# A hybrid block on one core: statistics by halves, W1 staged in W2's memory, weight peaks one per step, splits behind the tangents, and the first half's routing ahead of the last groups' additions

## The reference, cut to what matters

```
x = x + angles(layernorm(x))      # layer norm, l2 norm; s = clip(Q K^T) with 512 keys,
                                  # B = (1 - arccos(s)/pi)^9; l2norm(B @ q_weight) + bias
x = x + moe(layernorm(x))         # 8 experts of 128-512-128, top 2 of 8, plus a shared one, exact gelu
x = x + linear_attention(layernorm(x))   # 16 heads of 8, elu + 1
x = x + moe(layernorm(x))         # the same weights again
```

## Time and profile before

| what | us |
| --- | --- |
| median of 3 runs (lowest to highest) | 670.29 (667.02 to 672.75) |
| profiled execution: its time | 669.43 |
| its span, first to last instruction | 667.7 |
| busy in the span: PE / DVE / ACT / POOL | 489.1 / 515.2 / 450.7 / 366.1 |
| mean granted TensorE clock, as a share of full speed | 0.921 |

### The profile page before, as it was taken

The page is one execution under the profiler, slowest core; times in us unless marked ns, Lnnn a source line. Parts: engine busy times, 40 slices in busy tenths (PEclk is TensorE's granted clock), DMA queues, the critical chain, the costliest instruction groups (busy, mean ns, idle before and its releaser), DMA issues.

```text
span 667.7 us, 13526 instructions
## 1 busy us (share of the span) xinstructions
PE 489.1 (73%) x3817; PEld 354.5 (53%) x3817; DVE 515.2 (77%) x1200; ACT 450.7 (67%) x841; POOL 366.1 (55%) x382
## 2 busy tenths in 40 slices
PE   1276822874786987899957787866767999999770
PEld 1132302874332457788846566644332479999560
DVE  3988671588789547899889598776786769999992
ACT  1269999796562556899948578855642579999660
POOL 6023100333577777777747522237778737777673
PEclk9999975998698999899979999979896999999896
DMA  8800000004023453455581114102235324446943
GB/s 274 231 15 0 1 0 0 1 1 127 25 77 107 115 129 74 110 100 106 121 164 49 65 64 127 31 14 76 77 105 122 85 63 100 101 100 139 216 129 135
DMA packets 111961, 59.68 MB, mean 89 GB/s; under 512 B 76538, under 2 KB 101076, under 8 KB 111892
## 3 DMA queue, kind: packets, MB, share of 16 engines
q1 hardware_dynamic: 102804, 40.07, 25.2%
q0 software_dynamic: 9088, 18.76, 9.7%
HBM read 16.27 MB, written 23.90 MB: 60 GB/s over the span
## 4 chain that ended last, share of the span: by engine, by line
POOL 22%; issue 21%; DVE 16%; PE 16%; ACT 12%; SPq 9%; DMA 3%; POOLq 0%; DVEq 0%; ACTq 0%
POOL routed_rows L775 11%; POOL expert_results L821 6%; SPq L607 5%; SPq L616 2%; DMA side<-expert_results 2%; PE PA L1194 2%; DVE big L2084 2%; ACT SC L877 2%; DVE BN L1427 2%; DVE side L2098 2%; PE PA L1157 1%; DVE X L1645 1%; DVE peaks L1531 1%; SPq L605 1%; POOL RS L721 1%
## 5 line engine op out<-in xcount | busy, mean ns | idle before, releaser
L821 POOL DMA_INDIRECT expert_results<-side,DG x156 | 162.9, 1044 | 66.8 <-issue 47.0
L775 POOL DMA_INDIRECT routed_rows<-big,SLQ x128 | 143.1, 1118 | 57.2 <-issue 44.6
L1407 PE MATMUL PC<-W,big 128*128 x624 | 118.9, 277 | 27.5 <-DVE side L2098 27.1
L1097 ACT ACTIVATE SC<-PA,B1T,scl 128x256 f32<-128x256 f32 x208 | 100.8, 576 | 20.5 <-PE PA L1391 15.1
L2087 DVE SCALAR_TENSOR_TENSOR big<-SC,scl,big 128x1024 f16<-128x1024 f32 x78 | 100.2, 1284 | 2.8
L1409 PE MATMUL PC<-W,big 128*128 x468 | 87.6, 222 | 0.0
L1407 PEld LDWEIGHTS PC<-W,big 128*128 128x128 f16 x624 | 58.6, 99 | 38.7 <-issue 32.6
L2084 DVE TENSOR_SCALAR big<-SC,scl 128x1024 f16<-128x1024 f32 x78 | 67.4, 864 | 5.8 <-ACT SC L1097 5.8
L1107 ACT ACTIVATE big<-PC,DG 128x128 f32<-128x128 f32 x156 | 50.4, 390 | 19.3 <-PE PC L1407 10.4
L721 POOL TENSOR_TENSOR RS<-VA,halfneg 128x4 f32<-128x4 f32 x24 | 27.0, 1127 | 66.0 <-DVE VA L1679 65.9
L1097 ACT ACTIVATE SC<-PB,B1T,scl 128x256 f32<-128x256 f32 x104 | 50.7, 583 | 10.7 <-DVE big L2087 7.5
(11 more groups left out here) (288 smaller groups left out, 1188.7 us busy)
## 6 DMA issues: line engine op xcount, KB each, us to landing
big<-PB SPq DMA_DIRECT2D x32, 256.0 KB, 3.0
side<-expert_results SPq DMA_DIRECT2D x16, 512.0 KB, 4.1
routed_rows<-pad_zeros SPq DMA_DIRECT2D x23, 128.0 KB
expert_results<-side,DG POOLq DMA_INDIRECT x156
X<-n_L_attn_a_hidden_states SPq DMA_DIRECT2D x2, 1024.0 KB, 7.0
big<-in_L_ffn_w SPq DMA_DIRECT2D x1, 2048.0 KB, 8.4
routed_rows<-big,SLQ POOLq DMA_INDIRECT x128, 2.8
out_x<-X SPq DMA_DIRECT2D x8, 256.0 KB, 2.3
```

The costliest lines, as they stand in the source:

```text
L775: pool.indirect_dma_start(routed, bass.IndirectOffsetOnAxis(ap=SLQ[:, slot, t, c:c + 1], axis=0), XHL[:, slot, t, c, :].bitcast(I32), None ...
L821: pool.indirect_dma_start(results, bass.IndirectOffsetOnAxis(ap=DG[:, k, r, 0:1], axis=0), YT[:, k, r, :], None).then_inc(result_stored[k] ...
L1097: ins = act.activation(HF[:, k % 3, b * RU:(b + 1) * RU], up_out(k, b), ACT.Gelu, scale=INV1, bias=B1T[:, bass.ds(b1_at + b, 1)])
L1407: last = pe.matmul(both, hh, W2[:, :, at], start=(b == 0), stop=(b == HB - 1))
```

## The change

Nothing of what is computed changes. In the setup:

- K's weights are loaded ahead of X's second half, and POOL takes the inverse norms of K ahead of its last twelve constants. ACT loads its root table first of all.
- The first block's statistics are done by halves of 16 tiles: variances, first and second roots and the first two normalisations of half 0 come ahead of the statistics of X's second half; half 1's steps are spread over steps 1 to 4 of the score loop.
- The transposed K, attention weights and b1 are copied by ACT, out of other banks. W1 is staged in the memory where W2's parts will lie.

In the score loop the weight peaks come one per step (16 steps from step 3), and W1's splits leave it. Behind the last tangent DVE does the small peaks, the scales, W1's split and W2's split. POOL's reduction over partitions, and with it its bias additions, comes behind the peaks.

At the end of the value phase DVE does `choose(0)`, `place(0)` and `rows(0)` ahead of `first_add` of groups 6 and 7, and POOL puts single tiles of group 0's scatter between the roots and scalings of these groups. PE's and ACT's lists follow.

```
-        w1_stage = big[:, 0:WE]
+        w1_stage = W2[:].rearrange("p a n -> p (a n)").bitcast(F32)
...
                 sp.dma_start(grouped[:, mine, :, :], x_view[:, mine, :, :]).then_inc(s[name], 16)
-            sp.dma_start(KW[:], k_w.rearrange("(b p) d -> p b d", p=P)).then_inc(s["kw_loaded"], 16)
+                if not half:
+                    sp.dma_start(KW[:], k_w.rearrange("(b p) d -> p b d", p=P)).then_inc(s["kw_loaded"], 16)
...
-                    for g in range(NG - 1):
+                    for g in range(NG - 2):
                         x_scale(g)
                         group_root(g, 1)
+                    x_scale(NG - 2)
+                    scatter(0, 0, 0, (0,))
+                    group_root(NG - 2, 1)
+                    scatter(0, 0, 0, (1,))
                     x_scale(NG - 1)
-                    scatter(0, 0, 0, (0,))
+                    scatter(0, 0, 0, (2,))
                     group_root(NG - 1, 1)
-                    scatter(0, 0, 0, (1, 2, 3))
+                    scatter(0, 0, 0, (3,))
                     scatter(1, 0, 1)
...
+            act.preload_act_table(ACT.Abs_reciprocal_sqrt)
...
+            root(1)
+            act.wait_ge(s["setup_t"], 1)
+            act.activation(KT[:], PBk[0][:], ACT.Copy).then_inc(b_read[0], 1)
+            root(2)
             act.wait_ge(s["consts_made"], CONSTS)
-            root(1)
-            root(2)
+            act.wait_ge(s["setup_t"], 2)
+            act.activation(WOT[:], PA[1][:, 3 * P:4 * P], ACT.Copy).then_inc(s["wot_copied"], 1)
+            act.activation(WQKVT[:], PA[1][:, 0:3 * P], ACT.Copy).then_inc(a_read[1], 1)
+            act.wait_ge(s["setup_t"], 3)
+            act.activation(B1T[:], PA[0][:, 0:(E + 1) * HB], ACT.Copy).then_inc(a_read[0], 1)
...
             for n in range(NA + 3):
                 g = n // 2
-                if n == HI_AT:
-                    act.wait_ge(s["scales_made"], SCALE_STEPS)
-                if 0 <= n - HI_AT < CHUNKS // 2:
-                    weight_hi(n - HI_AT)
...
+                if n == 2:
+                    root(3)
                 score_angles(n - 3)
+                if n == 3:
+                    root(4)
...
                     act.preload_act_table(ACT.Gelu)
+                    gap(0)
                     gate_normalise(NG - 3)
                     gate_hi(NG - 3)
                     value_squares(NG - 1)
-                    gap(0)
+                    early_gelu(0)
+                    gate_turn(NG - 3)
                     gate_normalise(NG - 2)
                     gate_hi(NG - 2)
-                    gate_turn(NG - 3)
-                    early_gelu(0)
                     early_gelu(1)
...
                     route(0)
+                    early_up(0)
                     gate_rows_turn(NG - 3)
                     gate_logits(NG - 4)
-                    early_up(0)
                     early_up(1)
...
             for g in range(NG // 2):
                 bn(0, g)
+            variances(0)
             dve.wait_ge(s["kw_loaded"], 16)
             dve.wait_ge(s["k_rs"], 1)
...
+            first_roots(0)
+            second_roots(0)
...
+            for g in range(2):
+                normalise_a(g, 0, g)
+            dve.wait_ge(s["x_second"], 16)
+            for g in range(NG // 2, NG):
+                bn(0, g)
+            PEAKS_AT = 3
             for n in range(NA + 4):
                 g = n // 2
+                if n == 1:
+                    variances(1)
                 if n >= 4:
                     tangent(n - 4, (n - 4) // 4, (n - 4) % 4)
                 if n % 2 == 0 and 0 < g <= NG:
                     query(g - 1, (g - 1) // 2, (g - 1) % 2)
+                if n == 2:
+                    first_roots(1)
+                if n == 4:
+                    second_roots(1)
+                if n % 2 == 0 and 0 < g < NG - 1:
+                    normalise_a(g + 1, (g + 1) // 2, (g + 1) % 2)
+                if 0 <= n - PEAKS_AT < 2 * NG:
+                    largest_weight(n - PEAKS_AT)
+            small_peaks()
+            dve.wait_ge(s["peak_made"], 2 * NG)
+            dve.tensor_reduce(amax[:, 0:2], peaks[:], AX.X, ALU.max).then_inc(s["amax_made"], 1)
+            scales()
+            split_weights(W1H, W1L, w1_stage, S1, 0)
+            dve.wait_ge(s["w_split"], CHUNKS // 2)
+            split_weights(W2H, W2L, w2_stage, S2, CHUNKS // 2)
...
+                    gate_logits(NG - 5)
+                    choose(0)
                     sum_squares(NG - 2)
                     first_shift(NG - 3)
-                    gate_logits(NG - 5)
+                    place(0)
+                    rows(0)
                     first_add(NG - 2)
-                    choose(0)
+                    gate_lo(NG - 3)
                     sum_squares(NG - 1)
-                    gate_lo(NG - 3)
                     first_shift(NG - 2)
-                    place(0)
                     first_add(NG - 1)
-                    rows(0)
                     gate_logits(NG - 4)
```

More of the change, by code:

```diff
@@ L379, in build @@
         per = NG // 2
-        USES = [("setup", (0, 0), (1, 1), (1, 0)),
+        USES = [("setup", (1, 1), (1, 0), (0, 0)),
                 ("query", (0, 0), (per, per), (per, per)),
@@ L486, in build @@
         CONSTS, SCALE_STEPS, TABLE_STEPS, SMALL = 39, 10, 10, 10
-        def roots(norm):
-            return norm + 2
         xt_turned = [s[f"xt_turned{i}"] for i in range(RING)]
@@ L840, in _ @@
         def _(act):
+            act.preload_act_table(ACT.Abs_reciprocal_sqrt)
             def root(n):
+                tiles = slice((n - 1) // 2 * HT, ((n - 1) // 2 + 1) * HT)
                 act.wait_ge(s["var_ready"], n)
-                act.activation(EST[:], VA[:], ACT.Abs_reciprocal_sqrt).then_inc(s["root_ready"], 1)
+                act.activation(EST[:, tiles], VA[:, tiles], ACT.Abs_reciprocal_sqrt).then_inc(s["root_ready"], 1)
             act.wait_ge(s["kw_loaded"], 16)
@@ new lines, in step, with first_tiles, variances @@
+            def step(ins):
+                stat_steps[0] += 1
+                ins.then_inc(s["stat_step"], 1)
+                dve.wait_ge(s["stat_step"], stat_steps[0])
+            def first_tiles(half):
+                return slice(half * HT, (half + 1) * HT)
+            def variances(half):
+                h = first_tiles(half)
+                dve.wait_ge(s["bn_done"], (half + 1) * NG // 2)
+                m0, q0, m1, q1 = (BN[:, h, i] for i in (1, 2, 4, 5))
+                step(dve.tensor_tensor(MEAN[:, h], m0, m1, ALU.add))
+                step(dve.tensor_scalar(MEAN[:, h], MEAN[:, h], 0.5, None, ALU.mult))
+                step(dve.tensor_tensor(VAR[:, h], m0, m1, ALU.subtract))
+                step(dve.tensor_tensor(VAR[:, h], VAR[:, h], VAR[:, h], ALU.mult))
+                step(dve.tensor_tensor(VA[:, h], q0, q1, ALU.add))
+                step(dve.tensor_scalar(VA[:, h], VA[:, h], 1.0 / D, None, ALU.mult))
+                step(dve.scalar_tensor_tensor(VAR[:, h], VAR[:, h], 0.25, VA[:, h], ALU.mult, ALU.add))
+                step(dve.tensor_scalar(VA[:, h], VAR[:, h], LN_EPS, None, ALU.add))
+                dve.sem_inc(s["var_ready"], 1)
@@ new lines, in inverse_root, with first_roots @@
+            def inverse_root(h, n):
+                dve.wait_ge(s["root_ready"], n)
+                step(dve.tensor_tensor(VB[:, h], EST[:, h], EST[:, h], ALU.mult))
+                step(dve.tensor_tensor(VB[:, h], VB[:, h], VA[:, h], ALU.mult))
+                step(dve.tensor_scalar(VB[:, h], VB[:, h], -0.5, 1.5, ALU.mult, ALU.add))
+            def first_roots(half):
+                h = first_tiles(half)
+                inverse_root(h, 2 * half + 1)
+                step(dve.tensor_tensor(RS[:, h], EST[:, h], VB[:, h], ALU.mult))
+                step(dve.tensor_tensor(VA[:, h], RS[:, h], RS[:, h], ALU.mult))
+                step(dve.tensor_tensor(VA[:, h], VA[:, h], VAR[:, h], ALU.mult))
+                step(dve.tensor_scalar(VA[:, h], VA[:, h], 1e-12, None, ALU.add))
+                dve.sem_inc(s["var_ready"], 1)
@@ L1476, in normalise_to, with second_roots @@
+            def second_roots(half):
+                h = first_tiles(half)
+                inverse_root(h, 2 * half + 2)
+                step(dve.tensor_tensor(VB[:, h], EST[:, h], VB[:, h], ALU.mult))
+                step(dve.tensor_tensor(RS[:, h], RS[:, h], VB[:, h], ALU.mult))
             def normalise_to(rows, g):
```

117 lines of the change are left out of this document (22 added, 95 removed).

## The result

The changed kernel takes **651.86 us** (median of 4 runs, 650.00 to 654.83), the kernel before, measured beside it, 671.52 (4 runs, 667.02 to 674.00): a ratio of **0.972**, 95% interval 0.965 to 0.979. The profiled execution took 654.83 us (span 653.0), the slowest of its four; against the 667.7 of before its trace shows 14.7 us.

What follows compares the result with a forecast made beforehand. It took DVE to bound the setup, ACT the score loop, POOL's scatters the routed loop's stalls, then TensorE. Terms 10.3 + 2.6 − 5.5 + 3.8 = 11.2 us off 669.43 gave 658.2, stated as 659; range 650 to 666.

Steps and rivals of the forecast that it cites:

- The first score: Setup: the first score comes at 24.9 instead of 35.12, 10.3 us earlier (7.4 to 10.8).
- K's part: Setup: K's weights land at about 7.4 instead of 10.38; if not, everything behind moves by 2.9 us.
- The loop: Score loop: first to fifteenth score square takes 44.6 us against 47.2, a gain of 2.6 us (0.9 to 3.4).
- Behind the tangents: Between last tangent and first sum of squares: 5.5 us lost, from nothing to 9.
- The cost of the additions: Behind the tangents: POOL's eight bias additions, 9.9 us, take some 8 us from DVE's 16.8 of splits.
- the end of POOL's reduction: Behind the tangents: the reduction over partitions takes 0.5 to 4.8 us, nearer to the longer.
- the long end: POOL's reduction taking 4.8 us: the bias parts then end at 35.8 us, 7.1 late.
- the short end: POOL's reduction taking 0.5 us: the bias parts then end at 31.5 us, 2.8 late.
- Rival two: Behind the tangents: short reduction, and additions lag instead of DVE, so they cost nothing; 653 us, chance 0.15.
- The routing: End of value phase and routed loop: 7 us of stalls gone, 3.2 us lost on last addition; net 3.8 (0 to 6).
- 56 unbroken scatters keep that: Routing: POOL's second group of scatters starts 5.8 us earlier, and the scatters from there on preserve this lead.
- afterwards TensorE is the bound: Routed loop behind the stalls: TensorE, busy 55.00 of 55 us, sets the pace, so only the stall is gained.

Runs made afterwards that it cites:

- e7: Changed kernel with the load of K's weights put back behind the second half of X: 653.21 us, one run.
- e6: Changed kernel with the eight bias additions moved from POOL to DVE, plus one small POOL operation right behind its reduction: 649.50 us, ratio 0.971.
- e4: Changed kernel with four more small POOL operations between the last scatter and the first store of results in the first layer: 661.19 us, ratio 0.991.
- e12: Changed kernel measured again, unaltered, on another chip: 651.42 us, ratio 0.975.
- e5: Changed kernel measured again, unaltered, on another chip: 650.88 us, ratio 0.974.
- e3: Changed kernel with the eight bias additions taken from POOL and done by DVE, six behind the splits, two behind the first sum of squares: 656.64 us, ratio 0.984.
- e10: Changed kernel with eight extra matmuls on TensorE between the last arctangent and the first value product: 652.33 us, ratio 0.975.

## Why the prediction was right, and where it was not

**The first score: right.** 10.3 us forecast, 10.6 in the trace. Its parts held: K at 7.40 (7.4 forecast), the score at 24.49 (24.9). e7 bears out K's part, 2.5 us for the 2.9.

**The loop: right.** 2.6 forecast, 3.2 found. The first two pairs took 6.46 and 7.00 us (6.9 and 6.7 forecast), the others 6.03 to 6.23 (6.2). With a peak in every step these pairs take about as long as the 6.04 us of before.

**Behind the tangents: the mis-sized term.** 5.5 us were to be lost; 1.9 were (30.7 us between last tangent and first sum of squares, 28.75 before). The cost of the additions was right: the splits take 24.76 us instead of 16.8, so 8.0 as forecast (8, worked out from a loss of 2.06 us that by the rows is 2.04). They ran beside each other for 15.81 us, in which POOL did 9.9 us of additions (eight at the 1.24 of the earlier trace rows) and DVE 7.8 us of splits: 17.7 us of work in 15.8, as if the two had taken turns for all but 2 of them. By this much the rule of the Trainium skill weighed in the prediction (SBUF — State Buffer, section SBUF: two separate sides) is borne out. The step that failed is the end of POOL's reduction. I put it "nearer to the long end, since POOL waited for nothing else". DVE had its result after 0.42 us; POOL's pause of 7.4 us is paid by its own next instruction (e6), and nobody else waits for it. The 4.8 us of the long end were no wait for the reduction either: in between DVE waited for ACT and did a tangent and a query (timeline of the kernel before), and went on to the scales at 42.82 without a pause.

```profile
41.08 1.22 DVE L1585 SCALAR_TENSOR_TENSOR big<-SC,PA 128x1024 f32<-128x1024 f32 x1 [2.10 <-ACT SC L881]
```

With the short end the prediction's own sum was 31.5 us and 2.8 late; 30.7 and 1.9 were measured. This term makes 3.6 of the 3.7 us by which the trace's 14.9 up to the first combination exceed the 11.2.

**Rival two (653 us) gave the nearest time for the wrong reason**: the reduction did end soon, but the additions cost DVE the full 8 us. That 651.86 lies in the range at all it owes to the room left for rivals and scatter, and in part to luck.

**The routing: the net is near, its limit was misread.** 3.8 us forecast; 3.0, 4.1 and 4.8 in the three traces, up to the first combination. The last addition is 4.1 us later against the values (4.2 forecast: 172.6 for 168.43), the first shared split 2.7 (3.2), the first scatter 8.1 and the second group's 6.6 us sooner (8 and 5.8). But "56 unbroken scatters keep that" failed: they took 1.15 us each instead of 1.10, and the first store is only 4.0 us sooner against the values. The stalls therefore don't quite go. And I took TensorE for the bound behind them ("afterwards TensorE is the bound"): that was wrong, and its full busy row hid it, 53.00 of 53 us. What released the first combination is SP's list, which restarts when the last scatters have landed (e4): at 265.96 before, at 250.05, 250.49 and 250.53 in the three traces, 4.0, 3.6 and 3.6 us sooner against the values. From there to the load of the results it took 64.3 us before and 65.2, 64.3 and 62.9 after, which is most of the difference between 3.0, 4.1 and 4.8. Why single issues of SP take longer in one execution than in another, no row tells.

**Not in the forecast: layer 1.** I had it only move along. From the choice of its first half to that of its second it took 43.25 us before, 43.94 in the changed kernel and 41.51 in e12. The three windows of that stage, in this order (kernel before, changed kernel, e12):

```profile
434.98:478.23 43.25, 27.41 (x198) 18.69 (x196) 31.07 (x106) 23.49 (x42) 27.00 (x25) 0.80 0.19 58
```

```profile
420.03:463.97 43.94, 28.59 (x195) 18.23 (x193) 31.07 (x106) 23.49 (x42) 26.96 (x25) 0.79 0.18 57
```

```profile
418.25:459.76 41.51, 26.10 (x198) 17.43 (x196) 30.99 (x106) 23.48 (x42) 25.86 (x23) 0.84 0.18 57
```

The work is the same to 0.1 us on DVE and ACT; TensorE is busy for 27.41, 28.59 and 26.10 us at a granted clock of 0.80, 0.79 and 0.84, means over stretches at either level (1.2 and 2.4 GHz). The rest of the kernel gives e12 another 1.8 us (187.64 from there to the end, 189.47 before). Behind the first combination e12 gains 3.6 us on the kernel before and e5 2.1, while the first trace loses 0.2. Over all 14 traces the stage takes one of four lengths: 41.5 us in three, 43.2 in eight (the kernel before among them), 43.9 to 44.0 in two, 45.6 in one (e3). So the gain beyond the first combination is not shown to be the change's. Why executions of one program differ so, no run here tells.

## What to carry to other kernels

An operation given to POOL can cost DVE more than doing it: beside these splits, eight additions that DVE does in 5 us (e3) cost it 8. Two queues that run without a pause behind the same event keep the same distance, and a probe that delays one of them only shows that it has little slack: read what the last step waited for. Here SP's waits, not TensorE's busy share, said what released the first combination. A pause on an engine is charged to whoever waits for that engine next, so look who that is before it is counted.

## What the runs showed of the hardware that was not expected

POOL stands idle for 6.8 to 7.4 us before its first instruction behind a reduction over partitions (13 traces); in e3, where that instruction's input came 28 us later, it started 7.0 us behind the input. The result of the reduction is there 0.42 us after it begins. Four operations of 128x4 with a wait behind each took 8.1 us on POOL, where one between scatters took 1.04. The four matmuls of the first score took 1.98 us in e7 and e10 and 3.45 to 3.78 in the other executions of the changed setup, at a granted clock of 1.00 in the windows around them in each; no row tells why.
